# All data transfers issued by SyncE, x and its transpose loaded further ahead, one parameter word for ScalarE, and VectorE's parameter load one step earlier

## Chip, core and metric

The kernel runs on one core of a Trainium2 chip. The time is the device time of one execution in microseconds (us); below it stands as the median of three runs. The profile records one execution of its own.

## What is computed

There are B = 128 items. Each is a matrix x of 128 rows and 512 columns in 32-bit floats, and each goes through four residual stages. The per-item choices are a mask kind (0 to 2), a language (0 to 9), a category (0 to 63) and three scalars zX, zY, zR.

```
h = tanh(x @ W1 + b1); s = h @ v                    # one score for each row
p = softmax(s under the item's mask); x1 = x + (p @ x) / count
a = relu(x1 @ W1[lang] + b1[lang]) @ W2[lang] + b2[lang]
x2 = x1 + layernorm(x1 + a) * gamma[lang] + beta[lang]
x3 = x2 + zX*lap_columns(x2) + zY*lap_rows(x2) + zR*x2*(1 - x2)
out = x3 + x3 @ W[cat] + b[cat]
```

## The kernel before, in words

Every engine runs its own hand-written program of "slots". The loop is unrolled: `run_slots(slot, 0, B + 4)` calls `slot(s)` for s = 0 to 132, and inside one slot an engine works on several items at once, each at another stage (s, s - 1, ... s - 5). The items are sorted by category at the start, so that a category's weights `w3` (1 MB) are loaded only for the first item of a category (`cond=fresh`). Engines wait for each other with semaphores (`wait_ge`), and buffers are rings: three for the transposed x (`xts`), two for x (`xs`), for the category bias (`b3_wide`) and for most others.

**TensorE**, in slot T: the attention projection of item T (`attn_project`, L359), four pieces of the category product of item T - 5 (`category`, L426) with small products between them (L383, L388, L367), the pooling of T - 1 (L395), the transpose of x3 of item T - 4 (`x3_transpose`, L412), the adapter projection of T (L377) and the adapter's second product of T - 1 (`adapter_up`, L404).

**VectorE**, in slot T: `normalize` (L759) of T - 2, mask and row maximum of T, result of T - 5 (L752), `add_b2` (L789) and `add_beta` (L795) of T - 1, the adapter's sum `add_adapted` (L701), the mean (L707), the reaction product (L765), `add_identity` (L727, which TensorE's L388 waits for), columns (L772), epsilon (L744, needs ScalarE's variance L513), `center` (L735), and `add_rows` (L782), which makes x3.

**ScalarE** does tanh (L548), the variance (L513), relu (L529), exponentials (L498), copies, and in the kernel before it also issues three of the transfers: `load_xT` (L564), `load_x` (L578) and `load_b3` (L571). **SyncE** issues the constants (L248 to L253), three row shifts of x2 inside the on-chip memory (`shift_rows`, L276 to L278), the store of the result (L268) and `load_w3` (L262). A transfer waits in the queue of the engine that issues it (q1 is SyncE's, q10 ScalarE's).

SyncE's slot s starts when x2 of item s is there, which VectorE makes in its slot s + 2. SyncE's numbers therefore run two behind those of TensorE.

```
def load_params(eng, what, count, item):
    if item.is_first:
        eng.wait_ge(params_made, 2)
```

ScalarE loads 3 words for each item, VectorE 2, SyncE 4, TensorE twice 1.

Of the kernel before, what the change touches and what calls it, by code (L numbers as in the profile page):

```python
# [12 lines left out]
P = 128  # L13
# [3 lines left out]
FRESH, WSLOT, CAT, ITEM, LANG, KIND, NPARAM = 0, 1, 2, 3, 4, 5, 6  # L17
# [47 lines left out]
def cond_residual_kernel(nc, x, xT, ids, cols, w1a,  # L65
                         w1l, w2l, lrows, gamma, w3, b3, out):
    B, S, D = x.shape
    A = w1a.shape[1] // (D // P)
    K = D // P
# [18 lines left out]
    with ctx:  # L88
# [6 lines left out]
        gamma_wide = sb("gamma_wide", [P, L * D])  # L95
# [34 lines left out]
        xs = sb("xs", [P, 2, D])  # L130
# [115 lines left out]
        def _(sp):  # L246
# [5 lines left out]
            sp.wait_ge(xT_in[0], 16)  # L252
            sp.dma_start(gamma_wide[:, :], gamma.rearrange("l d -> (l d)").partition_broadcast(P)  # L253
                         ).then_inc(gamma_in, 16)

# [24 lines left out]

            words = {}

            def slot(s):
                if s.inside(B):
                    shift_rows(s)
                    words[(s).n] = load_params(sp, FRESH, 4, s)
                if (s - 3).inside(B):
                    store(s - 3, words[(s - 3).n][3])
                if s.inside(B):
                    load_w3(s, words[(s).n][2], words[(s).n][0], words[(s).n][1])  # L290
# [176 lines left out]
        def _(act):  # L467
# [91 lines left out]
            def load_xT(a, item):  # L559
                r = a.ring(3)  # L560
                if a.is_at_least(3):
                    act.wait_ge(xw_mm, a.upto(3))
                    act.wait_ge(attn_mm, a.upto(3))
                act.dma_start(xts[:, r], xT[bass.ds(item, 1)].rearrange("o p (k s) -> p (o k) s", k=K)  # L564
                              ).then_inc(xT_in[r], 16)

            def load_b3(c, cat):
                r = c.ring(2)
                if c.is_at_least(2):
                    act.wait_ge(res_ready, c.upto(2))  # L570
                act.dma_start(b3_wide[:, r], b3[bass.ds(cat, 1)].rearrange("o d -> (o d)").partition_broadcast(P)  # L571
                              ).then_inc(b3_in[r], 16)

            def load_x(d, item):
                r = d.ring(2)
                if d.is_at_least(2):
                    act.wait_ge(pool_mm, d.upto(2))
                act.dma_start(xs[:, r], x[bass.ds(item, 1)].rearrange("o s d -> s (o d)")).then_inc(x_in[r], 16)  # L578

            words = {}  # L580

            def slot(s):
                if s.is_first:
                    words[s.n] = load_params(act, CAT, 3, s)
                    load_xT(s, words[s.n][1])
                if (s + 1).inside(B):
                    words[(s + 1).n] = load_params(act, CAT, 3, s + 1)
                    load_xT(s + 1, words[(s + 1).n][1])
                if s.is_first:
                    load_x(s, words[s.n][1])  # L590
                    for i in range(4, L):
                        move_b2(i)
# [4 lines left out]
                if (s - 1).inside(B) and not (s - 1).is_first:  # L597
                    load_x(s - 1, words[(s - 1).n][1])
                if (s - 2).inside(B):
                    relu(s - 2, words[(s - 2).n][2])  # L600
# [10 lines left out]
                if (s - 4).inside(B):  # L611
                    load_b3(s - 4, words[(s - 4).n][0])
# [7 lines left out]
        def _(dve):  # L620
# [179 lines left out]
            def slot(s):  # L800
# [15 lines left out]
                if (s - 1).inside(B):  # L816
                    add_beta(s - 1, words[(s - 1).n][0])
                    add_adapted(s - 1)
                if (s + 1).inside(B):
                    words[(s + 1).n] = load_params(dve, LANG, 2, s + 1)  # L820
                if (s - 1).inside(B):
                    mean(s - 1)
# [145 lines left out]
```

## Time and profile before

| | us |
|---|---|
| median of 3 runs | 1063.28 (1061.41 to 1067.64) |
| the profiled execution's own time | 1065.58 |
| its span, first to last instruction | 1063.7 |
| TensorE busy (matmul) | 1040.2, 98% |
| VectorE busy | 918.9, 86% |
| ScalarE busy | 480.7, 45% |
| GpSimd busy | 528.2, 50% |

The span is about 2 us shorter than the execution's own time. Busy times leave out waiting and the sequencer's own work (register loads, issuing of transfers). TensorE's granted clock is full in all 40 slices of the page, and the 16 transfer engines moved 253 GB/s in the mean.

### The profile page before, as it was taken

The numbers are of one execution on the slowest core, as the hardware profiler recorded it, in microseconds if no ns is written. First come the engines' busy times: TensorE is split into PE (matmuls) and PEld (weight loads), VectorE is DVE, ScalarE is ACT, GpSimd is POOL, SyncE is SP. The second block draws the span as 40 slices with busy tenths as digits, with TensorE's granted clock in tenths as the row PEclk, the third lists the DMA queues.
The fourth block names the chain that finished last, engine by engine and source line by source line (L and its number), as shares of the span: only waits on it lengthen the run. The fifth ranks groups of instructions, "written<-read, shape, count | busy, mean of one in ns | idle before, by whom it ended". The sixth has DMA issues, their size and how long they took to land.

```text
span 1063.7 us, 22593 instructions
## 1 busy us (share of the span) xinstructions
PE 1040.2 (98%) x4784; PEld 639.1 (60%) x4784; DVE 918.9 (86%) x2216; ACT 480.7 (45%) x1422; POOL 528.2 (50%) x537
## 2 busy tenths in 40 slices
PE   5899999999999999999999999999999999999998
PEld 3566666656665566666665665666666666666663
DVE  5789888988898888988888898889988988988886
ACT  3444444444444444444444454444444444444452
POOL 3345445544544454554454454445454454454454
PEclk9999999999999999999999999999999999999999
DMA  8686898687878978767777778888787888897875
GB/s 332 218 261 212 270 289 258 210 270 231 276 247 263 312 240 264 245 208 240 226 251 223 239 236 254 253 279 279 249 266 254 270 241 275 280 279 235 276 224 176
DMA packets 119109, 268.82 MB, mean 253 GB/s; under 512 B 13010, under 2 KB 13028, under 8 KB 111556
## 3 DMA queue, kind: packets, MB, share of 16 engines
q1 hardware_dynamic: 63428, 166.24, 47.7%
q10 hardware_dynamic: 55552, 101.15, 31.2%
q8 instruction: 47, 0.77, 0.3%
q14 instruction: 82, 0.67, 0.2%
HBM read 243.21 MB, written 33.55 MB: 260 GB/s over the span
## 4 chain that ended last, share of the span: by engine, by line
PE 40%; issue 32%; POOL 21%; DVE 2%; POOLq 0%; ACTq 0%; DVEq 0%; ACT 0%
PE ps_out L426 17%; POOL b_wide L912 8%; POOL rows_near L905 8%; PE bank_hidden L377 5%; PE ps_attn L359 4%; PE ps_adapt L404 4%; PE ps_pool L395 4%; POOL rstd L891 4%; PE ps_x3T L412 2%; POOL neighbours L899 2%; DVE x L759 1%; PE bank_hidden L388 1%; PE bank_scores L367 1%; PE bank_scores L383 1%; DVE x L782 1%
## 5 line engine op out<-in xcount | busy, mean ns | idle before, releaser
L426 PE MATMUL ps_out<-w3s,x3T 128*128 x1016 | 491.7, 593 | 0.8 <-ACT x3T L492 0.8
L899 POOL TENSOR_TENSOR neighbours<-x 128x510 f32<-128x510 f32 x128 | 132.6, 1036 | 191.0 <-DVE x L759 191.0
L426 PEld LDWEIGHTS ps_out<-w3s,x3T 128*128 128x128 f32 x1016 | 164.1, 191 | 101.6 <-issue 101.5
L891 POOL TENSOR_TENSOR rstd<-var_eps,minus_half 128x1 f32<-128x1 f32 x128 | 70.1, 548 | 302.1 <-DVE var_eps L744 302.1
L905 POOL TENSOR_TENSOR rows_near<-rows_near 128x512 f32<-128x512 f32 x128 | 163.2, 1275 | 23.0 <-DMA rows_near<-x 23.0
L359 PEld LDWEIGHTS ps_attn<-xts,w_attn 128*128 128x128 f32 x1024 | 134.3, 191 | 60.8 <-issue 60.8
L912 POOL TENSOR_TENSOR b_wide<-b_wide,x 128x512 f32<-128x512 f32 x128 | 162.9, 1272 | 3.9 <-DMA b_wide<-in_b 3.9
L548 ACT ACTIVATE attn<-ps_attn,vals 128x128 f32<-128x128 f32 x128 | 47.0, 367 | 230.6 <-issue 159.5
L498 ACT ACTIVATE probs<-masked,neg_max 128x128 f32<-128x128 f32 x128 | 51.5, 402 | 216.0 <-DVE neg_max L694 215.9
L377 PE MATMUL bank_hidden<-w_all,xts 128*128 x1024 | 135.4, 275 | 0.1
L359 PE MATMUL ps_attn<-xts,w_attn 128*128 128x128 f32 x1024 | 135.0, 275 | 0.3 <-issue 0.3
L404 PE MATMUL ps_adapt<-w_all,hid 128*128 x256 | 131.2, 594 | 0.5 <-DVE x L759 0.4
L395 PE MATMUL ps_pool<-xs,mixT 128*128 128x512 f32 x256 | 130.7, 592 | 0.0
L377 PEld LDWEIGHTS bank_hidden<-w_all,xts 128*128 128x128 f32 x1024 | 124.5, 192 | 2.0 <-issue 2.0
L412 PEld LDWEIGHTS ps_x3T<-ident,x 128*128 128x128 f32 x512 | 61.3, 141 | 78.3 <-issue 40.5
L701 DVE SCALAR_TENSOR_TENSOR ps_adapt<-ps_adapt,x_b 128x512 f32<-128x512 f32 x128 | 88.9, 694 | 19.6 <-PE ps_adapt L404 18.6
L538 ACT ACTIVATE ps_react<-x,c_t,nzr_t 128x512 f32<-128x512 f32 x128 | 97.8, 764 | 3.8 <-DVE x L782 3.8
L735 DVE SCALAR_TENSOR_TENSOR ps_adapt<-ps_adapt,neg_mean,gamma_wide 128x512 f32<-128x512 f32 x128 | 97.0, 758 | 1.5
L759 DVE SCALAR_TENSOR_TENSOR x<-ps_adapt,rstd,x_beta 128x512 f32<-128x512 f32 x128 | 95.4, 745 | 1.1 <-POOL rstd L891 1.0
L782 DVE SCALAR_TENSOR_TENSOR x<-rows_near,wide_rows,ps_react 128x512 f32<-128x512 f32 x128 | 94.5, 738 | 1.5 <-POOL rows_near L905 1.4
L772 DVE SCALAR_TENSOR_TENSOR ps_react<-neighbours,wide_rows,ps_react 128x512 f32<-128x512 f32 x128 | 95.5, 746 | 0.1
L765 DVE TENSOR_TENSOR ps_react<-ps_react,x 128x512 f32<-128x512 f32 x128 | 88.2, 689 | 0.9 <-ACT ps_react L538 0.9
(111 smaller groups left out, 1306.4 us busy)
## 6 DMA issues: line engine op xcount, KB each, us to landing
w3s<-in_w SPq DMA_DIRECT2D x128, 1024.0 KB
rows_near<-x SPq DMA_DIRECT2D x256, 252.0 KB
xts<-in_xT ACTq DMA_DIRECT2D x128, 256.0 KB, 4.3
xs<-in_x ACTq DMA_DIRECT2D x128, 256.0 KB, 4.5
b_wide<-in_b ACTq DMA_DIRECT2D x128, 256.0 KB, 4.5
out_x<-res SPq DMA_DIRECT2D x128, 256.0 KB, 4.5
w_all<-in_w1l SPq DMA_DIRECT2D x1, 2560.0 KB, 10.4
w_all<-in_w2l SPq DMA_DIRECT2D x1, 2560.0 KB, 16.4
```

Source lines behind the costliest of these rows:

```text
L359: mm = pe.matmul(ps_attn, w1_attn[:, k * A:(k + 1) * A], xts[:, r, k, :], start=(k == 0), stop=(k == K - 1))
L377: mm = pe.matmul(ps_xw, xts[:, s.ring(3), k, :], w1_all[:, bass.ds(lang * (K * A) + k * A, A)], start=(k == 0), stop=(k == K - 1))
L395: pe.matmul(ps_pool[:, :], mixT[:, d.ring(2), :], xs[:, d.ring(2), :], start=True, stop=True).then_inc(pool_mm, 1)
L404: pe.matmul(ps_adapt[:, :], hid[:, g.ring(2), :], w2_all[:, bass.ds(lang * D, D)], start=True, stop=True).then_inc(adapt_mm, 1)
L426: mm = pe.matmul(out_bank(j)[:, :], x3T[:, j.ring(2), k * P:(k + 1) * P], w3s[:, bass.ds(wslot * (K * D) + k * D, D)], start=(k == 0), sto ...
L538: nc.scalar.activation(ps_react[:, :], x2[:, h.ring(2), :], ACT.Identity, bias=c0_t[:, bass.ds(h.n, 1)], scale=nzr_t[:, bass.ds(h.n, 1)]). ...
L759: nc.vector.scalar_tensor_tensor(x2[:, q, :], normed[:, :], rstd[:, q:q + 1], x1_beta[:, q, :], ALU.mult, ALU.add).then_inc(x2_ready, 1)
L782: nc.vector.scalar_tensor_tensor(x3[:, q, :], above[:, q, :], zy_t[:, bass.ds(i.n, 1)], ps_react[:, :], ALU.mult, ALU.add).then_inc(x3_rea ...
L891: nc.gpsimd.tensor_tensor(rstd[:, q:q + 1], var_eps[:, q:q + 1], minus_half[:, :], ALU.pow).then_inc(rstd_ready, 1)
L899: nc.gpsimd.tensor_tensor(neighbours[:, q, 1:D - 1], x2[:, q, 0:D - 2], x2[:, q, 2:D], ALU.add).then_inc(neighbours_ready, 1)
L905: nc.gpsimd.tensor_tensor(above[:, q, :], above[:, q, :], below[:, q, :], ALU.add).then_inc(rows_ready, 1)
L912: nc.gpsimd.tensor_tensor(b3_wide[:, q, :], b3_wide[:, q, :], x3[:, q, :], ALU.add).then_inc(x3_b3_ready, 1)
```

## The change

SyncE now issues every transfer apart from the two constants at the head of ScalarE's program. `load_xT`, `load_b3` and `load_x` move to SyncE with their waits unchanged. SyncE loads its four words six items ahead, the transposed x five of its own slot numbers ahead (three of TensorE's) and x three ahead (one of TensorE's). The `gamma` load (2.5 MB, waits for the first transposed x) comes behind the first six parameter loads, and the transposed x of item 2 and x of item 1 are issued behind `gamma`. ScalarE loads one word (the language) instead of three, two items ahead and behind the variance. VectorE's load of two words moves from behind `add_adapted` to ahead of it.

```diff
@@ SyncE
-            sp.wait_ge(xT_in[0], 16)
-            sp.dma_start(gamma_wide[:, :], gamma.rearrange("l d -> (l d)").partition_broadcast(P)
-                         ).then_inc(gamma_in, 16)
...
+            def load_xT(a, item):
+                r = a.ring(3)
+                if a.is_at_least(3):
+                    sp.wait_ge(xw_mm, a.upto(3))
+                    sp.wait_ge(attn_mm, a.upto(3))
+                sp.dma_start(xts[:, r], xT[bass.ds(item, 1)].rearrange("o p (k s) -> p (o k) s", k=K)
+                              ).then_inc(xT_in[r], 16)
+
+            def load_b3(c, cat):
+                r = c.ring(2)
+                if c.is_at_least(2):
+                    sp.wait_ge(res_ready, c.upto(2))
+                sp.dma_start(b3_wide[:, r], b3[bass.ds(cat, 1)].rearrange("o d -> (o d)").partition_broadcast(P)
+                              ).then_inc(b3_in[r], 16)
+
+            def load_x(d, item):
+                r = d.ring(2)
+                if d.is_at_least(2):
+                    sp.wait_ge(pool_mm, d.upto(2))
+                sp.dma_start(xs[:, r], x[bass.ds(item, 1)].rearrange("o s d -> s (o d)")).then_inc(x_in[r], 16)
+
             words = {}
+            for i in range(6):
+                words[i] = load_params(sp, FRESH, 4, Step(i))
+                if i < 2:
+                    load_xT(Step(i), words[i][3])
+                if i == 0:
+                    load_x(Step(i), words[i][3])
+            sp.wait_ge(xT_in[0], 16)
+            sp.dma_start(gamma_wide[:, :], gamma.rearrange("l d -> (l d)").partition_broadcast(P)
+                         ).then_inc(gamma_in, 16)
+
+            load_xT(Step(2), words[2][3])
+            load_x(Step(1), words[1][3])
+            load_xT(Step(3), words[3][3])
+            load_x(Step(2), words[2][3])
+            load_xT(Step(4), words[4][3])
 
             def slot(s):
                 if s.inside(B):
                     shift_rows(s)
-                    words[(s).n] = load_params(sp, FRESH, 4, s)
+                if (s + 5).inside(B):
+                    load_xT(s + 5, words[(s + 5).n][3])
+                if (s + 3).inside(B):
+                    load_x(s + 3, words[(s + 3).n][3])
+                if (s - 1).inside(B):
+                    load_b3(s - 1, words[(s - 1).n][2])
                 if (s - 3).inside(B):
                     store(s - 3, words[(s - 3).n][3])
+                if (s + 6).inside(B):
+                    words[(s + 6).n] = load_params(sp, FRESH, 4, s + 6)
                 if s.inside(B):
                     load_w3(s, words[(s).n][2], words[(s).n][0], words[(s).n][1])
@@ ScalarE (its own load_xT, load_b3, load_x are removed)
             def slot(s):
                 if s.is_first:
-                    words[s.n] = load_params(act, CAT, 3, s)
-                    load_xT(s, words[s.n][1])
-                if (s + 1).inside(B):
-                    words[(s + 1).n] = load_params(act, CAT, 3, s + 1)
-                    load_xT(s + 1, words[(s + 1).n][1])
-                if s.is_first:
-                    load_x(s, words[s.n][1])
+                    words[s.n] = load_params(act, LANG, 1, s)
+                    words[(s + 1).n] = load_params(act, LANG, 1, s + 1)
                     for i in range(4, L):
                         move_b2(i)
                 if (s - 1).inside(B):
                     attn_tanh(s - 1)
                 if (s - 3).inside(B):
                     variance(s - 3)
-                if (s - 1).inside(B) and not (s - 1).is_first:
-                    load_x(s - 1, words[(s - 1).n][1])
+                if (s + 2).inside(B):
+                    words[(s + 2).n] = load_params(act, LANG, 1, s + 2)
                 if (s - 2).inside(B):
-                    relu(s - 2, words[(s - 2).n][2])
+                    relu(s - 2, words[(s - 2).n][0])
...
-                if (s - 4).inside(B):
-                    load_b3(s - 4, words[(s - 4).n][0])
@@ VectorE
                     add_beta(s - 1, words[(s - 1).n][0])
-                    add_adapted(s - 1)
                 if (s + 1).inside(B):
                     words[(s + 1).n] = load_params(dve, LANG, 2, s + 1)
+                if (s - 1).inside(B):
+                    add_adapted(s - 1)
                 if (s - 1).inside(B):
                     mean(s - 1)
```

## Rows read from the trace of the kernel before

**Rows 1.** The page: busy us of each engine (share) and instructions

```profile
PE 1040.2 (98%) x4784; PEld 639.1 (60%) x4784; DVE 918.9 (86%) x2216; ACT 480.7 (45%) x1422; POOL 528.2 (50%) x537
```

**Rows 2.** Timeline (start, us, engine, line): four starts of TensorE's slots

```profile
50.04 1.05 PE L359 MATMUL ps_attn<-xts,w_attn 128*128 128x128 f32 x8
...
501.23 1.05 PE L359 MATMUL ps_attn<-xts,w_attn 128*128 128x128 f32 x8
...
509.17 1.05 PE L359 MATMUL ps_attn<-xts,w_attn 128*128 128x128 f32 x8
...
1028.43 1.05 PE L359 MATMUL ps_attn<-xts,w_attn 128*128 128x128 f32 x8
```

**Rows 3.** Waits of the whole span: us in total, times, longest us

```profile
ACT attn L548 <- issue: 159.5, 77, 3.1
...
DVE neg_mean L707 <- issue: 33.9, 28, 1.5
...
DVE var_eps L744 <- ACT square_junk L513: 26.2, 57, 1.2
...
SPq L262 <- PE ps_out L426: 292.3, 126, 3.4
```

**Rows 4.** All parameter loads (L238): ns min/median/max, first and last start

```profile
L238 PEldq TENSOR_LOAD <-all_params x256: 293/298/493, 20.9 to 1054.7; - x128
L238 ACTq TENSOR_LOAD <-all_params x128: 698/1374/2881, 14.6 to 1012.5; - x128
L238 DVEq TENSOR_LOAD <-all_params x128: 522/1080/2589, 21.3 to 1028.6; - x128
L238 SPq TENSOR_LOAD <-all_params x128: 816/1531/2757, 36.9 to 1049.6; - x128
```

**Rows 5.** Timeline of an ordinary slot

```profile
508.34 0.67 DVE L795 TENSOR_TENSOR x_beta<-ps_pool,beta_wide 128x512 f32<-128x512 f32 x1
...
509.37 0.70 DVE L701 SCALAR_TENSOR_TENSOR ps_adapt<-ps_adapt,x_b 128x512 f32<-128x512 f32 x1 [0.35 <-PE ps_adapt L404]
...
510.51 0.15 DVE L707 TENSOR_SCALAR neg_mean<-y_sum 128x1 f32<-128x1 f32 x1 [0.39 <-DVE ps_adapt L701]
...
513.02 0.74 DVE L782 SCALAR_TENSOR_TENSOR x<-rows_near,wide_rows,ps_react 128x512 f32<-128x512 f32 x1
...
514.48 0.14 PEld L412 LDWEIGHTS ps_x3T<-ident,x 128*128 128x128 f32 x1 [0.24 <-issue]
```

**Rows 6.** Timeline of a long slot

```profile
73.99 0.67 DVE L795 TENSOR_TENSOR x_beta<-ps_pool,beta_wide 128x512 f32<-128x512 f32 x1
...
74.58 0.69 DVE L701 SCALAR_TENSOR_TENSOR ps_adapt<-ps_adapt,x_b 128x512 f32<-128x512 f32 x1
...
76.70 0.15 DVE L707 TENSOR_SCALAR neg_mean<-y_sum 128x1 f32<-128x1 f32 x1 [1.37 <-issue]
```

**Rows 7.** The long slot's VectorE parameter load

```profile
L238 DVEq TENSOR_LOAD <-all_params x1: 2471/2471/2471, 74.2 to 74.2; - x1
```

**Rows 8.** Stretches: us, busy per engine (PE, PEld, DVE, ACT, POOL), clock, DMA share, GB/s

```profile
507.00:508.00 1.00, 1.00 (x11) 1.00 (x10) 1.00 (x3) 0.98 (x3) 1.00 (x2) 1.00 0.00 0
508.00:509.00 1.00, 1.00 (x7) 0.69 (x6) 1.00 (x3) 0.86 (x3) 1.00 (x2) 1.00 0.56 184
```

**Rows 9.** Timeline of the start

```profile
19.09 0.33 SPq L253 DMA_DIRECT2D gamma_wide<-in_gamma  x1
...
21.82 0.34 ACTq L564 DMA_DIRECT2D xts<-in_xT  x1
...
30.38 1.05 PE L359 MATMUL ps_attn<-xts,w_attn 128*128 128x128 f32 x8
...
32.75 0.76 DVE L735 SCALAR_TENSOR_TENSOR ps_adapt<-ps_adapt,neg_mean,gamma_wide 128x512 f32<-128x512 f32 x1
```

**Rows 10.** Transfers of 14 to 30 and 20 to 24 us: KB, us to landing

```profile
gamma_wide<-in_gamma SPq DMA_DIRECT2D x1, 2560.0 KB, 9.9
...
xts<-in_xT ACTq DMA_DIRECT2D x1, 256.0 KB, 7.5
```

More of the change, by code:

```diff
@@ L557, in column_ends @@
                                      ).then_inc(edges_ready, 1)
[L559 to L578, printed above, removed]
             words = {}
```

## The prediction

> **What bounds the kernel now.** I read the page first. TensorE's matmuls are busy for 98% of the span, VectorE for 86% and ScalarE for 45% [rows 1]. That says that TensorE is close to the bound, not how close. So the second view is the timeline at the starts of TensorE's slots. An ordinary slot is 509.17 - 501.23 = 7.94 us, and in it the matmuls follow each other without a gap. From the start of slot 5 (50.04) to that of slot 127 (1028.43) there are 122 slots in 978.4 us. At 7.935 each they would take 968.1 [rows 2]. The excess is 10.3 us, and that is all that any change to waits can win in the steady state. What lies before 50.04 and behind 1028.43 is the ramp and the tail.
>
> The third view is the waits. TensorE's gaps come from VectorE's results (mixT for L388, x3 for L412). What holds VectorE is not an engine: 28 times the mean (L707) waited with the cause "issue", 33.9 us in all, up to 1.5, and ScalarE's tanh did so 77 times, 159.5 us [rows 3]. The fourth view says what the sequencers did then. A parameter load takes VectorE 0.52 us at best, 1.08 in the median and 2.59 at worst, ScalarE's three words 0.70, 1.37 and 2.88, while TensorE's single word takes 0.30 nearly always [rows 4]. The last view is an ordinary slot beside a long one. In the ordinary one the sum (L701) starts at 509.37, when TensorE has delivered, and the mean at 510.51 [rows 5]. In the long one the sum starts at 74.58, but the mean only at 76.70, after a load of 2.47 us [rows 6, 7]. The long slots follow the long loads, and those fall where the transfer engines are full. So the kernel is bound by TensorE plus 10.3 us in which a register load holds VectorE, or ScalarE, too long.
>
> **ScalarE's part.** It loses three transfers for each item and two of three words, and its load moves behind the variance, where the next instruction (relu) waits for TensorE anyway. Tanh and variance then start when their data are there. This ends most of the wait of epsilon for the variance, 26.2 us in 57 waits [rows 3]. No row shows one word on ScalarE. Its bounds are TensorE's 0.30 from below and three words' 1.37 from above; I take 0.5, since TensorE's row has the same count. The cover is over 1 us in an ordinary slot, so it costs nothing. At 1.37 or more, without that cover, relu would be up to 0.4 late, and its reader (`adapter_up`) comes 2 us later still.
>
> **VectorE's part.** The load before stood behind the sum and ran beside it. Two cases have to be told apart.
>
> Case one, VectorE waits for TensorE (ordinary slot). Before, the load started with the sum at 509.37, so the mean came at 509.45 + d for a load of length d, and at 510.16 without a stall (a sum and its accumulator read, 0.79). Now the load starts with L795 at 508.34, and everything up to the wait is cover.
>
> Case two, VectorE is behind (long slot). The sum followed L795 by 0.59, the load began at 74.2 and the mean stood idle for 1.37 us after a load of 2.47 [rows 6, 7], that is d - 1.1. Now the sum itself stands behind the load and begins at about d + 0.1 instead of 0.59 after L795. The stall is d - 0.5, so it is 0.6 us worse than before.
>
> The cover now: VectorE's busy time for each item is 918.9 / 128 = 7.18 us, of which a little belongs to the set-up; with 7.1 a slot of 7.94 leaves 0.8 for a stall, so loads up to 0.8 + 0.5 = 1.3 us cost nothing. Lateness is carried on: a slot starts late by what the last left over, plus d, minus 1.3, never under zero. TensorE notices when the lateness passes some limit. In the ordinary slot x3 is finished at 513.02 + 0.74 = 513.76 and its reader loads weights at 514.48 [rows 5], with a mean that was 0.35 late already, so the limit is 0.72 + 0.35, about 1.05 us.
>
> What d will be is the open number. It starts up to 1 us earlier than now. At 507 to 508 the transfer engines are idle, and at 508 to 509 they are at 0.56 [rows 8], so the load mostly runs before the row shifts and `w3` fill them. With a quiet engine 0.52 is shown, so ordinary loads should be some 0.7. Where a new category's weights follow at once on those of the last, the engines are full throughout, and nothing shortens it: up to 2.59. I take 1.5 for those with `w3` in flight. Then one such load is 0.2 late, a following ordinary one makes up 0.6, and only runs of several reach the limit. Remaining excess: at best 0; with today's lengths kept (ordinary loads 1.08 recover 0.2, long ones of 1.8 to 2.5 lose 0.5 to 1.2) about what it was, 8 to 10. I take 3, nearer to the lower end as the load leaves the full stretch. Gain 10.3 - 3 = 7.3 us, bounds 10.3 and 0.
>
> **SyncE in the steady state.** It gains three issues, each 0.34 us plus 0.1 for addresses and waits: 1.4 us a slot, and its load of up to 2.76 [rows 4] stays. It waits for the category product before issuing `w3` for 292.3 us in 126 slots, 2.3 each [rows 3]. The 1.4 us fit, so `w3` and the shifts behind it are issued when they were. Passed are: shifts first, then transposed x, x, bias, store, parameters, `w3`. The transposed x is needed two TensorE slots after its issue (about 15 us), x and bias over 6; even the one caught beside `gamma` took 7.5 [rows 10]. Cost zero, with that cover; without it each late microsecond would be TensorE's.
>
> **The start.** Here the change costs. Before, `gamma` was issued at 19.09, transposed x of item 2 at 21.82 in the other queue [rows 9]; they landed at 19.09 + 9.9 = 29.0 and 21.82 + 7.5 = 29.3 [rows 10]. TensorE took the latter at 30.38 and VectorE gamma at 32.75 [rows 9]. Now SyncE runs six loads of four words first. From 14.6, when ScalarE's first load starts [rows 4]: 6 x 0.9 (0.82 is SyncE's minimum; the queue is nearly idle) and three issues of 0.4 give 14.6 + 5.4 + 1.2 = 21.2, with one or two loads slowed by traffic 22. `gamma` lands at 22 + 9.4 = 31.4 (half a microsecond shorter, as nothing shares with it), before 32.75. The transposed x of item 2 stands in the same queue behind it, 0.7 us more: about 32.1, 1.7 later than 30.38. Everything behind is a chain (tanh of item 2 stands ahead of item 0's variance on ScalarE), so I carry 1.7 in full. Below: loads at the minimum and half of it made up in the ramp, 0.5. Above: loads at the median 1.53 give `gamma` 4 us later, so 5. In the ramp VectorE is behind and its load costs 0.3 more a slot, ScalarE's shorter load gives as much back: zero.
>
> From the Trainium skill, "DMA: Bandwidth & Descriptors", section "Queues, rings and completion order": each transfer engine takes a queue's descriptors in order and alternates between queues packet by packet. By alternation the small transfer of item 2 should have passed `gamma` by far, and here it landed 0.3 behind it; by the first half of the rule it now stands wholly behind `gamma`, as I have it. The sum would be 1.7 us smaller if the queue did not keep order.
>
> **The tail.** The same semaphores order the last shifts, biases and stores, and the last product is TensorE's. Zero, bounds -0.8 (no bias load beside the last shift) and +0.5.
>
> **Sum.** -7.3 + 1.7 = -5.6 us. The profiled execution's own time is 1065.58, its span 1063.7; the median of the runs is 1063.28, within 2.3 of the first. The excess does not depend on that difference, so 1063.3 - 5.6 = 1057.7, say 1058.
>
> **Rivals.** *The load is no shorter (A).* It starts later again whenever VectorE is late, and then meets the full engines as now. Excess left 8, start +1.7: 1063.3 - 2.3 + 1.7 = 1062.7. For it: 1.08 in the median with engines at 0.56 share. Against: 0.52 is shown where they are quiet.
>
> *Slower: the sum behind the load makes VectorE the bound (B).* A slot of VectorE alone is 7.1 + d - 0.5. It passes 7.94 at a mean d of 1.34, and each 0.1 above costs 122 x 0.1 = 12 us. At a mean of 1.4 it is 7 us over the floor, plus 5 for the unevenness, with the start 1063.3 - 10.3 + 12 + 1.7 = 1066.7; at 1.45, 1073. For it: loads of 2.5 us exist, and nothing covers them now. Against: the median is 1.08, and each late start only reaches today's phase.
>
> *A heavy start (C).* SyncE's loads take 1.5 us: 1063.3 - 7.3 + 5 = 1061.
>
> *All gaps close (D).* 1063.3 - 10.3 + 0.5 = 1053.5.
>
> *It does nothing (E).* The Trainium skill, same page, section "Issuing engines are not separate DMA queues", says that issuing from several engines saves only the sequencer's time to issue, mostly small. By that ScalarE's three issues were never in the way. As a mechanism here: 3 x 0.34 us on an engine that is busy 45%, all hidden, and the start alone counts: 1063.3 + 1.7 = 1065.
>
> **Numbers.** Forecast 0.42, A 0.2, B 0.12, C 0.08, D 0.13, E 0.05. The range 1053 to 1067 takes in the forecast's own bounds (1054 to 1061), A, C, D, E and half of B. A measurement of this kernel tells some 0.5% (5.3 us) from nothing, so faster is under 1058.0: all of D, most of half the forecast, some of C and A's luck, 0.42 x 0.65 + 0.13 + 0.04 = 0.44; slower is over 1068.6: part of B, 0.1; the rest, 0.46.
>
> **What the profile will show.** Right: slot starts of TensorE at 7.94 with few over 8.2; "issue" gone from tanh; the mean no longer waiting for issue, the sum doing so at times instead; VectorE's median load well under 1.08; epsilon's wait for the variance gone; `gamma` issued near 22, attention of item 2 near 32. Wrong if VectorE's loads stay at 1.1 or more with the sum idle behind them in most slots, if L426 waits for `w3`, or if slot 5 starts later than 52.

## The result, and the profile after

The changed kernel took 1053.32 us in the median of 7 runs (1052.18 to 1058.22). The kernel before took 1067.39 (1061.41 to 1068.84, 7 runs) beside it. The ratio is 0.9889, with a 95% interval from 0.9862 to 0.9916: the change makes the kernel 1.1% faster. (The ratio is estimated from all the runs; the two medians alone give 0.9868, inside the interval.) The profiled execution has a span of 1051.6 us, 12.1 less than before.

The page's busy line hardly moves against [rows 1]. TensorE's 1031.5 is 8.7 lower, and its share of the span is 98% as before:

```profile
PE 1031.5 (98%) x4784; PEld 641.8 (61%) x4784; DVE 913.4 (87%) x2216; ACT 487.7 (46%) x1422; POOL 531.0 (50%) x537
```

TensorE's slot starts in the timeline (start, us, engine, line), the answer to [rows 2]:

```profile
48.61 1.05 PE L398 MATMUL ps_attn<-xts,w_attn 128*128 128x128 f32 x8
...
500.86 1.05 PE L398 MATMUL ps_attn<-xts,w_attn 128*128 128x128 f32 x8
...
1017.20 1.05 PE L398 MATMUL ps_attn<-xts,w_attn 128*128 128x128 f32 x8
```

From slot 5 to slot 127 it is 1017.20 - 48.61 = 968.6 us. At 7.935 a slot, 122 slots take 968.1, so the excess is 0.5 us, where it was 10.3. The difference of the spans comes apart in three: -9.8 us in the steady state, -1.4 before slot 5 (50.04 to 48.61), -0.9 behind the start of slot 127 (35.3 to 34.4).

The waits of the whole span (us, times, longest), the answer to [rows 3]:

```profile
ACT attn L587 <- PE ps_attn L398: 142.7, 123, 1.2
...
DVE ps_adapt L712 <- PE ps_adapt L443: 62.5, 118, 0.5
...
DVE var_eps L755 <- ACT square_junk L552: 1.3, 2, 0.7
...
SPq L258 <- PE ps_out L465: 167.2, 120, 3.1
```

Tanh waits for TensorE now, in 123 slots, and never for issue. The mean's wait for issue is gone from the view, and so is all but 1.3 us of epsilon's wait for ScalarE. SyncE still waits 1.4 us a slot for the category product (before 2.3).

The parameter loads, the answer to [rows 4]:

```profile
L238 PEldq TENSOR_LOAD <-all_params x256: 294/299/535, 20.3 to 1042.8; - x128
L238 SPq TENSOR_LOAD <-all_params x128: 295/878/1919, 14.4 to 996.9; - x128
L238 ACTq TENSOR_LOAD <-all_params x128: 276/285/1998, 14.4 to 994.6; - x128
L238 DVEq TENSOR_LOAD <-all_params x128: 522/532/1597, 20.7 to 1015.8; - x128
```

VectorE's median fell from 1.08 to 0.53, ScalarE's from 1.37 to 0.28. An ordinary slot in the timeline, the answer to [rows 5], now with ScalarE's rows, for they turn out to be what counts:

```profile
500.86 1.05 PE L398 MATMUL ps_attn<-xts,w_attn 128*128 128x128 f32 x8
...
501.95 0.37 ACT L587 ACTIVATE attn<-ps_attn,vals 128x128 f32<-128x128 f32 x1 [1.19 <-PE ps_attn L398]
502.21 0.68 ACT L552 ACTIVATE square_junk<-ps_adapt,neg_mean 128x512 f32<-128x512 f32 x1
...
503.78 0.15 DVE L755 TENSOR_SCALAR var_eps<-var_sum 128x1 f32<-128x1 f32 x1
...
504.50 0.74 DVE L793 SCALAR_TENSOR_TENSOR x<-rows_near,wide_rows,ps_react 128x512 f32<-128x512 f32 x1
...
506.17 0.14 PEld L451 LDWEIGHTS ps_x3T<-ident,x 128*128 128x128 f32 x1 [0.24 <-issue]
```

Reckon from the slot's start, 500.86. Tanh runs at 1.09, at once when attention is done. The square follows, epsilon runs at 2.92, x3 is finished at 505.24, and TensorE reads it at 5.31, so 0.93 us lie between. (The fillers of the next section measure a margin of 1.1.)

Now the long slot of the kernel before again [rows 6], with ScalarE's rows, which the prediction had not looked at, first its register load and then the timeline:

```profile
L238 ACTq TENSOR_LOAD <-all_params x1: 2757/2757/2757, 74.1 to 74.1; - x1
```

```profile
74.40 0.39 ACT L522 ACTIVATE mix<-probs,scale 128x128 f32<-128x128 f32 x1
...
77.09 0.34 ACTq L564 DMA_DIRECT2D xts<-in_xT  x1
...
77.54 0.37 ACT L548 ACTIVATE attn<-ps_attn,vals 128x128 f32<-128x128 f32 x1 [2.74 <-issue]
...
77.81 0.68 ACT L513 ACTIVATE square_junk<-ps_adapt,neg_mean 128x512 f32<-128x512 f32 x1
...
78.61 0.15 DVE L744 TENSOR_SCALAR var_eps<-var_sum 128x1 f32<-128x1 f32 x1 [0.30 <-ACT square_junk L513]
...
80.23 0.42 PEld L412 LDWEIGHTS ps_x3T<-ident,x 128*128 128x128 f32 x4 [0.87 <-DVE x L782]
```

ScalarE's load began at 74.1 and took 2.76 us. Then came the issue of the transposed x, and only then, 3.70 behind the slot's start (73.84), tanh. Epsilon started at 4.77, held by the square and not by the late mean of [rows 6]. TensorE stood idle for x3, and the slot took 8.64 us.

Epsilon's start behind TensorE's slot start, slot by slot for slots 5 to 125, can be set against what the slot's length is over 7.935, the excess. Worked out from the traces of five kernels, three of them of the next section, that gives one table (us):

| epsilon starts at | before | VectorE's load alone | ScalarE's load alone | transfers alone | changed |
|---|---|---|---|---|---|
| under 4.0: slots, excess in all | 92, -0.1 | 83, -0.1 | 116, 0.0 | 113, 0.0 | 121, 0.5 |
| 4.0 to 4.2: slots, mean excess | 10, 0.07 | 12, 0.07 | 5, 0.12 | 7, 0.11 | none |
| 4.2 to 4.4 | 6, 0.24 | 8, 0.24 | none | 1, 0.28 | none |
| over 4.4 | 13, 0.63 | 18, 0.62 | none | none | none |

Up to 4.0 us nothing happens; beyond, the slot gets longer by about what epsilon starts later than that. In the kernel before the 29 late slots make up the whole excess: 0.7 + 1.4 + 8.3 = 10.4 us. The 0.5 us that the changed kernel keeps have another chain. They lie in slots 110 and 111, where GpSimd, which makes `rstd` from epsilon, had waited 3.12 us for a row shift to land and 1.74 us for the bias, so that VectorE waited for it:

```profile
887.92 0.75 DVE L770 SCALAR_TENSOR_TENSOR x<-ps_adapt,rstd,x_beta 128x512 f32<-128x512 f32 x1 [1.84 <-POOL rstd L903]
```

### The profile page after: what moved, and what is told of

Its sections match the earlier page's. It is cut to its first block and busy times, and to the rows that moved or that the text cites. A ratio compares the mean times of both kernels' runs of the same rounds, so it can differ in the third digit from the quotient of the medians.

```text
span 1051.6 us, 22463 instructions
## 1 busy us (share of the span) xinstructions
PE 1031.5 (98%) x4784; PEld 641.8 (61%) x4784; DVE 913.4 (87%) x2216; ACT 487.7 (46%) x1422; POOL 531.0 (50%) x537
## 5 line engine op out<-in xcount | busy, mean ns | idle before, releaser
L924 POOL TENSOR_TENSOR b_wide<-b_wide,x 128x512 f32<-128x512 f32 x128 | 162.7, 1271 | 44.3 <-DMA b_wide<-in_b 44.1
L917 POOL TENSOR_TENSOR rows_near<-rows_near 128x512 f32<-128x512 f32 x128 | 163.2, 1275 | 38.7 <-DMA rows_near<-x 38.3
L568 ACT ACTIVATE hid<-bank_hidden,vals 128x128 f32<-128x128 f32 x128 | 47.0, 368 | 245.3 <-PE bank_hidden L427 245.2
L537 ACT ACTIVATE probs<-masked,neg_max 128x128 f32<-128x128 f32 x128 | 51.6, 403 | 139.6 <-DVE neg_max L705 139.6
L451 PEld LDWEIGHTS ps_x3T<-ident,x 128*128 128x128 f32 x512 | 63.7, 141 | 69.2 <-issue 65.1
```

What stands on the lines that cost most here:

```text
L917: nc.gpsimd.tensor_tensor(above[:, q, :], above[:, q, :], below[:, q, :], ALU.add).then_inc(rows_ready, 1)
L924: nc.gpsimd.tensor_tensor(b3_wide[:, q, :], b3_wide[:, q, :], x3[:, q, :], ALU.add).then_inc(x3_b3_ready, 1)
```

## The experiments

All ratios are to the kernel before, run on the same chip in the same session, so the medians of different sessions are not to be compared. The kernel before had a median of 1067.39 us beside the first run of the changed kernel, 1069.46 beside the two kernels with one load moved, the one with both and the one with all but VectorE's load, 1069.30 beside the second run of the changed kernel, the transfers alone, the one word and gamma last, and 1065.22 beside the fillers and the transposed x behind the square. "Excess" is TensorE's time from slot 5 to slot 127, less 968.1, in the profiled execution.

| kernel | median us | ratio (95%) | excess | start of slot 5 | slot 127 to end |
|---|---|---|---|---|---|
| before, as in the profile of rows 2 | 1063.28 | 1 | 10.3 | 50.0 | 35.3 |
| changed, first | 1053.32 | 0.9889 (0.9862 to 0.9916) | 0.5 | 48.6 | 34.4 |
| changed, again | 1055.43 | 0.9875 (0.9847 to 0.9902) | -0.1 | 52.4 | 34.4 |
| VectorE's load alone | 1070.09 | 1.000 (0.998 to 1.002) | 13.9 | 53.6 | 35.2 |
| ScalarE's load alone | 1056.81 | 0.9869 (0.9841 to 0.9897) | 0.5 | 51.8 | 35.0 |
| both loads, not the transfers | 1056.36 | 0.9873 (0.9847 to 0.9899) | 0.2 | 51.0 | 35.2 |
| transfers alone | 1056.20 | 0.9885 (0.9857 to 0.9912) | 1.0 | 49.9 | 34.4 |
| all but VectorE's load | 1057.35 | 0.9879 (0.9851 to 0.9906) | 1.8 | 51.3 | 34.4 |
| one word in front of tanh | 1054.98 | 0.9873 (0.9845 to 0.9900) | 1.3 | 49.5 | 34.4 |
| gamma last | 1054.88, one run | - | -0.1 | 50.7 | 34.4 |
| filler in front | 1079.83 | 1.0128 (1.0100 to 1.0156) | 22.5 | 51.9 | 36.2 |
| longer filler in front | 1240.80 | 1.1647 (1.1615 to 1.1678) | 175.0 | 54.5 | 40.5 |
| filler behind tanh | 1097.87 | 1.0313 (1.0283 to 1.0344) | 40.7 | 49.7 | 36.3 |
| transposed x behind the square | 1062.17 | 0.9971 (0.9954 to 0.9988) | 3.9 | 56.1 | 35.1 |

**VectorE's load alone** (kernel before, one move):

```diff
                     add_beta(s - 1, words[(s - 1).n][0])
-                    add_adapted(s - 1)
                 if (s + 1).inside(B):
                     words[(s + 1).n] = load_params(dve, LANG, 2, s + 1)
+                if (s - 1).inside(B):
+                    add_adapted(s - 1)
```

> The kernel before with one edit: VectorE's parameter load stands ahead of the adapter's sum; ScalarE keeps its three words and its transfers. Theory P (place): a load is slow where it meets the row shifts and the category weights, which start to move some 1.3 us after their issue, so the early load is short, 0.53 us in the median as in the changed kernel, the mean no longer waits, and 6 to 8 of the 10.3 us of excess between slot 5 and slot 127 go; ratio 0.992 to 0.994. Theory O (overlap): the loads of ScalarE, VectorE and SyncE hinder each other, as they start within half a microsecond. VectorE's then comes first and is short too: the same here. Rival of my prediction (the sum stands behind a long load): median 1.1 or more, excess 8 or more, ratio 1.0 or above. In all three ScalarE's three words stay at 1.37 and epsilon still waits for the variance in some slots.

It gives nothing. The waits of this kernel show why:

```profile
ACT attn L548 <- issue: 162.4, 77, 3.5
...
DVE var_eps L744 <- ACT square_junk L513: 54.1, 55, 1.9
```

The mean's wait for issue is gone, and epsilon waits for ScalarE instead, 54.1 us where it was 26.2. VectorE comes to epsilon earlier (3.02 us behind the slot's start in the median, before 3.14; 3.25 at the 90th percentile, before 3.93), and epsilon starts hardly earlier in the median and later at the 90th percentile (3.21 and 4.63; before 3.26 and 4.44). The load's length changed as well: in the 43 slots in which it ran beside ScalarE's alone its median was 0.88 us, in the 61 in which nothing ran beside it 0.54. Theories P and O both had 6 to 8 us of excess going with this move; none went, and both fall here as accounts of the loss.

**ScalarE's load alone.** In the kernel before, its load of three words moves behind the variance (an item further ahead); nothing else.

```diff
                 if s.is_first:
                     words[s.n] = load_params(act, CAT, 3, s)
                     load_xT(s, words[s.n][1])
-                if (s + 1).inside(B):
                     words[(s + 1).n] = load_params(act, CAT, 3, s + 1)
+                if (s + 1).inside(B):
                     load_xT(s + 1, words[(s + 1).n][1])
...
                     variance(s - 3)
+                if (s + 2).inside(B):
+                    words[(s + 2).n] = load_params(act, CAT, 3, s + 2)
```

> The kernel before with one edit: ScalarE's load of three words goes behind the variance and one item further ahead; its transfers and VectorE's load stay. Theory P: VectorE's load stays at 1.08 in the median with a maximum over 2.3, and of the 10.3 us of excess some 3 go (tanh and variance on time). Theory O: VectorE's load loses its neighbour of 0.27 us ahead and falls to 0.6 to 0.8 in the median, and 7 or more of the excess go.

This one edit gives the whole gain. Tanh starts at 1.09 in the median (before 2.19), and epsilon's wait is down to 1.3 us in 2 times. The next row is as bad as ever and costs nothing:

```profile
DVE neg_mean L709 <- issue: 42.7, 34, 1.6
```

Neither theory had this. P had only 3 us going, and O had them go because VectorE's load would get shorter; its median was 1.20 us, longer than before.

**Both loads, without the transfers**, and **all but VectorE's load** (the changed kernel with that load behind the sum again, the first diff turned round):

> The kernel before with both loads moved (ScalarE's three words behind the variance, VectorE's ahead of the sum), and every transfer left where it was. If the loads alone hold VectorE and TensorE back, as both theories P and O say, the excess falls under 1.5 us and the ratio is 0.989 to 0.991, within the interval of the changed kernel. If moving the transfers to SyncE has a share of its own in the steady state (theory T), 2 us or more of excess stay. The start (slot 5 at 50.0) and the tail (35.3) should stay as before, as their gain of 1.4 and 0.9 us is put down to the transfers.

> The changed kernel with VectorE's load put back behind the adapter's sum; one word on ScalarE, all transfers on SyncE. Here ScalarE's load starts 1 us behind VectorE's and SyncE's 2.5 us behind, so nothing overlaps it. Theory P: its place meets shifts and weights as before, median 1.0 to 1.1, up to 2.5, the mean waits for issue in some 20 to 30 slots, 4 to 7 us of excess come back; ratio to the kernel before 0.993 to 0.996. Theory O: the load stays at 0.53, excess under 1.5 and ratio 0.988 to 0.990, as for the changed kernel.

The first has 0.2 us of excess, so theory T, which kept 2 us or more for the transfers, falls. The second has 1.8: VectorE's load is at 0.88 us again and the mean waits 44.8 us for issue in 34 waits, much as P said, but the 4 to 7 us that P had coming back do not come. The medians of these two and of ScalarE's load alone lie within 1.0 us, so VectorE's load is worth less than what these runs tell apart. Nor do the transfers have to move.

**The changed kernel again, and the transfers alone.** For the second, ScalarE's load of three words stands ahead of tanh again and VectorE's behind the sum; SyncE issues the transfers.

```diff
+                if (s + 2).inside(B):
+                    words[(s + 2).n] = load_params(act, CAT, 3, s + 2)
                 if (s - 1).inside(B):
                     attn_tanh(s - 1)
...
-                if (s + 2).inside(B):
-                    words[(s + 2).n] = load_params(act, LANG, 1, s + 2)
```

> The changed kernel itself once more, beside the next three, so that its ratio to the kernel before is known with one chip's runs: 0.988 to 0.990 is expected by all theories, some 10 to 12.5 us below the kernel before. In the profile the steady state from slot 5 to slot 127 should be within 1 us of 122 x 7.935 = 968.1 again. Open is how far the start to slot 5 (48.6 there, 50.0 to 53.6 in five other profiles) repeats: theory C (chance) says that it comes out anywhere from 48.5 to 51.5, theory S (the earlier issue of gamma and of the transposed x) that it stays under 49.

> All transfers issued by SyncE as in the change, but ScalarE's load of three words ahead of tanh and VectorE's load behind the sum, as before: the transfers' part of the change alone. Theory L (the gain is the removal of ScalarE's register load from in front of tanh and variance): the excess over 7.935 us a slot comes back to 8 to 14 us, and only the shorter tail (-0.8) and perhaps a shorter start are left: ratio 0.997 to 1.001. Theory T (the transfers on one queue, six slots of words ahead, do part of it, because ScalarE then has three issues less in the way): half of the 10 us of excess goes, ratio about 0.994.

The first repeats the gain (0.9875, excess -0.1). Its slot 5 starts at 52.4, so theory S falls, and the spread by chance is wider than C had it.

The second result overthrew my theory L, and T had half of it only. The transfers alone give all of the gain too, with ScalarE's load just as long as before and VectorE's at 0.88 in the median (before 1.08):

```profile
L238 ACTq TENSOR_LOAD <-all_params x128: 702/1350/3529, 14.5 to 995.5; - x128
L238 DVEq TENSOR_LOAD <-all_params x128: 524/878/2429, 21.5 to 1019.2; - x128
```

The waits of this kernel:

```profile
DVE neg_mean L718 <- issue: 36.1, 28, 1.7
...
DVE var_eps L755 <- ACT square_junk L552: 4.2, 11, 0.8
```

So the load as such is no fault. The same slot 8 in this kernel's timeline starts at 73.71, with a load of 2.66 us on ScalarE from 73.7 and one of 2.20 on VectorE:

```profile
76.49 0.37 ACT L587 ACTIVATE attn<-ps_attn,vals 128x128 f32<-128x128 f32 x1 [2.07 <-issue]
76.75 0.68 ACT L552 ACTIVATE square_junk<-ps_adapt,neg_mean 128x512 f32<-128x512 f32 x1
...
77.70 0.15 DVE L755 TENSOR_SCALAR var_eps<-var_sum 128x1 f32<-128x1 f32 x1
```

Tanh comes at 2.78 instead of 3.70 and epsilon at 3.99 instead of 4.77, just on the limit, and the slot takes 7.99 us. The 0.92 us that tanh gained are 0.57 because no transfer is issued between the load's end and tanh (0.67 us before, 0.10 now), 0.25 because the load starts earlier (over all slots half a microsecond: at -0.55 from the slot's start in the median, before -0.04; the issues of x and of the bias, which stood ahead of it in ScalarE's program, are gone), and 0.1 because it is shorter. That suggested a margin rather than a culprit (theory M): anything that takes some 0.8 us away ahead of the square should do.

**One word in front of tanh.** The changed kernel, with ScalarE's `load_params` of one word moved ahead of `attn_tanh`.

> The changed kernel, but ScalarE's load of one word stands at the head of its slot ahead of tanh, where the three words stood before. Theory N (the length counts: three words of 1.4 us in the median, up to 2.9, are too long there, one word is not): the one word takes 0.3 to 1.1 us, tanh starts that much later, the slack of a slot takes it, excess 0 to 2 us, ratio 0.988 to 0.991. Theory P (the place counts: what stands ahead of tanh meets the traffic of w3 and holds the chain from tanh over variance to x3 whatever it loads): loads of over 1.5 us in slots with fresh w3, excess over 4 us, ratio 0.992 or more.

N is right: loads of 0.49 in the median and 1.39 at most, started at -0.56, delay tanh hardly ever (1.09 in the median and at the 90th percentile), and no time is lost.

**Fillers.** One more ScalarE copy in each slot puts a number on the margin.

```diff
+                if (s - 4).inside(B):
+                    act.wait_ge(w1_in, 16)
+                    nc.scalar.activation(idle_junk[:, :], w1_all[:, 0:2560], ACT.Copy)
                 if (s - 1).inside(B):
                     attn_tanh(s - 1)
```

> The changed kernel with one more ScalarE instruction in each slot from the fourth: a copy of 2560 columns that nobody reads, ahead of tanh. Its price is estimated from the rows of 512 columns (575 ns) and 128 (276 ns): 2.2 us. Theory M (margin: a slot gets longer only by what epsilon starts later than 4.0 us behind the slot's start): ScalarE is free at -0.1, so tanh starts at 2.1 instead of 1.09, the square ends at 3.1 instead of 2.1, epsilon starts near 3.2: below the limit, so the excess from slot 5 to 127 stays under 2 us and the time within 2 us of the changed kernel's (ratio 0.986 to 0.991). Theory E (each microsecond ahead of tanh lengthens the chain from attention to x3): 122 slots by up to 1.0 us, over 20 us more, ratio over 1.005.

> The same with 4096 columns, estimated at 3.4 us. Theory M: tanh starts at 3.3, the square ends at 4.35, epsilon starts near 4.4, which is 0.35 to 0.4 past the limit in every slot: 122 times that is 43 to 49 us, ratio 1.025 to 1.04. Theory R (it is the register loads that hurt, by holding a sequencer while transfers are in flight, not ScalarE being late): ScalarE is busy 45% and takes 3.4 us more without loss, ratio under 0.995.

> The copy of 2560 columns between tanh and the square instead of ahead of tanh. Theory V (it is the square, and through it epsilon, that comes late): tanh starts at 1.09 as in the changed kernel, the square ends at about 1.4 + 2.2 + 0.9 = 4.45, epsilon starts near 4.5, 0.4 to 0.5 past the limit in every slot: 50 to 60 us more, ratio 1.035 to 1.05. Theory H (it is tanh, for which TensorE's attention scores wait): nothing changes against the changed kernel, ratio under 0.995.

The copies took 2.33 and 3.61 us. The last of the three in the timeline, one slot and the start of the next:

```profile
504.51 1.05 PE L399 MATMUL ps_attn<-xts,w_attn 128*128 128x128 f32 x8
505.60 0.37 ACT L588 ACTIVATE attn<-ps_attn,vals 128x128 f32<-128x128 f32 x1
...
505.87 2.33 ACT L611 ACTIVATE idle_junk<-w_all 128x2560 bf16<-128x2560 f32 x1
...
508.09 0.68 ACT L553 ACTIVATE square_junk<-ps_adapt,neg_mean 128x512 f32<-128x512 f32 x1
...
508.89 0.15 DVE L759 TENSOR_SCALAR var_eps<-var_sum 128x1 f32<-128x1 f32 x1 [1.17 <-ACT square_junk L553]
...
510.52 0.42 PEld L452 LDWEIGHTS ps_x3T<-ident,x 128*128 128x128 f32 x4 [0.93 <-DVE x L797]
...
512.77 1.05 PE L399 MATMUL ps_attn<-xts,w_attn 128*128 128x128 f32 x8
```

Tanh is on time at 1.09, the square is late, epsilon starts at 4.38, and the slot takes 8.26 us, 0.33 over. Theory V stands and H falls: it is the square and not tanh. V's figure of 50 to 60 us more was too high, as epsilon came at 4.38 and not at 4.5; it was some 40. R, by which ScalarE would take the longer filler without loss, falls with a ratio of 1.165. The three fillers measure the limit, if a slot gets longer by just what epsilon is past it. With epsilon at 4.23, 4.38 and 5.51 in the median the mean slot was 0.18, 0.33 and 1.43 us over, so the limit is 4.05, 4.05 and 4.08.

What failed was my estimate of where the filler in front would start. I had ScalarE free at -0.1. In fact tanh started at 3.17 and 4.45, so both fillers began at 0.94. A late epsilon makes VectorE's row maximum late (6.69 us behind the slot's start in the median, changed kernel 5.28), ScalarE's exponentials wait for that (305 us in all, changed kernel 139.6), and the delay comes round to the next slot's head. So the first filler, which M had below the limit, came past it, and the total agrees with theory E's figure of over 20 us. What speaks against E are the kernel with one word in front and the transfers alone, where up to a microsecond and more ahead of tanh costs next to nothing. With the longer filler TensorE also waited for tanh itself (attention scores, 108.8 us in 124 times), so the 4.08 of that kernel is no clean reading of the limit; the other two have 1.1 us of this wait at most.

**The transposed x behind the square** (kernel before, one move):

```diff
                 if (s + 1).inside(B):
                     words[(s + 1).n] = load_params(act, CAT, 3, s + 1)
-                    load_xT(s + 1, words[(s + 1).n][1])
...
                     variance(s - 3)
+                if (s + 1).inside(B):
+                    load_xT(s + 1, words[(s + 1).n][1])
```

> The kernel before with one edit: ScalarE issues the transposed x behind the variance instead of between its load of three words and tanh; everything else, VectorE's load too, stays. In the kernel before tanh starts 0.85 us after the end of the load, in the one with the transfers alone moved 0.3 after it. Theory M: tanh and the square come 0.5 us earlier; of the 30 slots of the kernel before in which epsilon started after 4.0 (mean 0.35 past it, up to 1.0) most fall under the limit, and the excess falls from 10 to 14 us to 2 to 4: ratio 0.990 to 0.993. Theory Q (the loads' lengths and the queue decide, not half a microsecond of issuing): ratio 0.998 to 1.002.

The excess is 3.9, inside M's range: tanh's median is 1.49 (before 2.19), and only 2 slots have epsilon after 4.0, where it was 29. They give 0.5 us of the excess; the other 3.3 lie in slots with epsilon in time. In the longest of these, 0.99 over at 733.3, GpSimd had waited 4.5 us for a row shift and VectorE 1.0 for GpSimd's `rstd`, as in the changed kernel's slots 110 and 111; for the others the cause stays open. The ratio of 0.9971 is neither M's (0.990 to 0.993) nor Q's (0.998 to 1.002). The edit has a price at the start, which I had overlooked: slot 5 starts at 56.1, 6.1 later than before and outside the 48.6 to 53.6 of the ten profiles above the fillers in the table. The transposed x of item 1 is issued later, beside gamma, and TensorE waits for it:

```profile
20.46 0.34 ACTq L564 DMA_DIRECT2D xts<-in_xT  x1
...
28.60 1.65 PE L359 MATMUL ps_attn<-xts,w_attn 128*128 128x128 f32 x6 [4.68 <-DMA xts<-in_xT]
```

**Gamma last.** The changed kernel with the transposed x of item 2 and x of item 1 issued ahead of gamma.

```diff
+            load_xT(Step(2), words[2][3])
+            load_x(Step(1), words[1][3])
             sp.dma_start(gamma_wide[:, :], gamma.rearrange("l d -> (l d)").partition_broadcast(P)
                          ).then_inc(gamma_in, 16)
-            load_xT(Step(2), words[2][3])
-            load_x(Step(1), words[1][3])
```

> The changed kernel with the transposed x of item 2 and x of item 1 issued ahead of gamma at the start. If one queue's transfers are served in the order of issue, the transposed x of item 2 lands about 4 to 5 us earlier than its 29.30 and gamma some 0.6 to 1 us later than 28.62; if they share the engines packet by packet, hardly anything moves. For the time both say nothing measurable: in the profile of the changed kernel TensorE took that item at 29.34, right behind its own work, so that nothing waited, and VectorE takes gamma only after 31: within 1 us of the changed kernel in the start to slot 5, apart from chance.

Two stretches of its transfers (KB, us to landing):

```profile
xts<-in_xT SPq DMA_DIRECT2D x1, 256.0 KB, 2.6
...
gamma_wide<-in_gamma SPq DMA_DIRECT2D x1, 2560.0 KB, 11.0
```

Ahead of gamma the small transfer, issued at 20.30, lands at 22.95, 6.35 us earlier than behind it (29.30). So the queue does work in order of issue, in this one run. Gamma, issued at 21.16 and so 1.4 later, lands at 32.2, 3.6 later than in the changed kernel, which is more than I had expected. The start to slot 5 (50.7) is in the middle of the others.

## Why the prediction came out as it did

The time lay in the range given, and 1.1% is on the "faster" side. But the likeliest forecast, -5.6 us, was half of the -12.1 between the profiles. The steady state went by rival D, to which I had given 0.13. The measured 1053.32 is 0.3 us above the lower end of the range, and the sum behind the forecast came true in neither term. The -7.3 us were the worth of VectorE's shorter load, and that move alone is worth nothing (ratio 1.000, 0.998 to 1.002). The +1.7 us of the start came out as -1.4. That the time still fell in the range, on the right side, was luck as far as this mechanism goes: the change also had the move that counts, and I had named it without a price. Point by point:

**The view of what bounds the kernel.** The 10.3 us of excess as the most that waits can give was right: 9.8 came back, and 10.4 in a second profile of the changed kernel. Wrong was the step from the third and fourth view, "in which a register load holds VectorE, or ScalarE, too long", for I then priced VectorE's half only. The load on VectorE held the mean 33.9 us in 28 waits, and that is unpaid: with 36.1 and 42.7 us of the same wait the excess is 1.0 and 0.5. The row that named the cause was in [rows 3] too, epsilon waiting for the square, 26.2 us in 57 times. I mentioned it as a by-product of "ScalarE's part" and gave it no term.

**Case two and the cover.** "Lateness is carried on", with its 3 us of remaining excess, was mis-sized; 0.5 and -0.1 were measured. The limit I had derived for it, 1.05 us over the ordinary slot, was good: epsilon ordinarily starts at 2.92 to 2.93 and the fillers put the limit at 4.05 to 4.08, 1.1 later. It applies to epsilon, whoever makes it late.

**The lengths of the loads.** VectorE's I put at 0.7 in ordinary slots and 1.5 with `w3` in flight. It was 0.53 in nearly all. "The engines are full throughout, and nothing shortens it" fails: at 1.06 us behind the issue of `w3` the transfer engines were 0.7 busy in the median and the load was at its minimum. ScalarE's one word took 0.28 in the median, under my lower bound of 0.30, and 2.0 at most, over my upper one of 1.37. It did cost nothing, as said, even in front of tanh.

**SyncE in the steady state.** Right: zero. Its wait for the category product shrank by 1.0 us a slot, of the 1.4 that I had charged, and some of the rest went into shorter loads (0.88 in the median, before 1.53). Not foreseen: GpSimd waits 44.1 us for the bias, 53 times (before 3.9, once), and 38.3 for the shifted rows (before 23.0). In the profile of the changed kernel this costs only the 0.5 us of slots 110 and 111.

**The start.** Wrong in size and sign. Gamma was issued at 19.78 and not near 22; rows of the changed kernel's timeline:

```profile
19.78 0.34 SPq L306 DMA_DIRECT2D gamma_wide<-in_gamma  x1
20.32 0.33 SPq L282 DMA_DIRECT2D xts<-in_xT  x1
...
29.35 1.16 PE L398 MATMUL ps_attn<-xts,w_attn 128*128 128x128 f32 x8
...
31.83 0.76 DVE L746 SCALAR_TENSOR_TENSOR ps_adapt<-ps_adapt,neg_mean,gamma_wide 128x512 f32<-128x512 f32 x1
```

The six loads took 0.49, 0.89, 0.31, 0.87, 0.29 and 0.87 us, 3.7 together, where I had taken 0.9 each from SyncE's minimum in [rows 4]. From there the reckoning held: gamma took 8.8 us to land (9.4 forecast), the transposed x landed at 29.30, 0.7 behind it as said, and TensorE's matmul took it at 29.35 with no gap behind the one before; only its weight load had waited, 0.85 us. How much of the -1.4 belongs to the change can't be told. In the ten profiles above the fillers in the table slot 5 starts at 48.6 to 53.6, and the changed kernel itself did so at 48.6 and 52.4. In the second of these TensorE's granted clock was 0.50 (1.2 GHz) from 23.0 to 27.7, in the kernel with gamma last 1.00 (2.4 GHz) from 22 to 30. So "slot 5 later than 52" was no sign of this change: the changed kernel has it both ways.

The order of the queue was as I had used it, and the kernel with gamma last shows it (the small transfer lands 6.35 us earlier when issued ahead of gamma): this agrees with the first half of the rule cited from the Trainium skill, "DMA: Bandwidth & Descriptors", section "Queues, rings and completion order".

**The tail.** I had zero with -0.8 as the bound. It is 0.6 to 0.9 shorter in all six kernels in which SyncE issues the transfers and no filler runs (34.4, against 35.0 to 35.3 in the five others). The cause wasn't looked for.

**The rivals.** A falls with VectorE's load at 0.53. B, VectorE as the bound, needed a mean load of 1.34 us, which never came. C, a heavy start, falls with 3.7 us for SyncE's six loads. E had looked at ScalarE's issues. The Trainium skill, same page, section "Issuing engines are not separate DMA queues", says that issuing from several engines saves only the sequencer's time, which is usually small beside the transfer. These runs agree: with the transfers left on ScalarE the gain is the same, and an issue takes 0.34 us where a transfer takes 4.5. What E made of it fails. I had priced 3 x 0.34 us on an engine that is busy 45% as hidden; taking them away alone gives 1.15% (0.9885, 0.9857 to 0.9912), because they stood ahead of the square, whose margin was used up. Small beside the transfer isn't small beside a margin.

In sum, what the runs show: in 29 of the 121 slots of the kernel before, ScalarE's queue of load, issue, tanh and square ended too late for epsilon, and those slots were 0.36 us too long in the mean. Moving the load takes 1.4 us out of that queue in the median, moving the transfers 0.9 in slot 8, and either is enough alone. They don't add up, because beyond the limit there is nothing left to win. No version tried is faster than the changed kernel by more than these runs can tell: the ratios of the changed kernel and five others lie between 0.9869 and 0.9889, with intervals that overlap, and the smallest edit among them is the move of ScalarE's load.

## What to carry to other kernels

Price a wait by the chain that ends in the bounding engine, and not by its own length: set the start of each link against the bounding engine's slot start, for all slots, and look for the point from which the slot gets longer. Here 34 us of idle VectorE cost nothing, and the whole loss of 10 us stood behind another wait of 26 us. Where several edits take time out of one queue, the first may bring all of the gain, as here.

## What the runs showed of the hardware

The length of a register load depends on more than its words. Four words took SyncE 0.82 at least in the kernel before and 0.29 to 0.89 at the start of the changed one. ScalarE's three words, at the same place, took 2.31 us in the median of the 53 slots in which fresh `w3` was on its way and 1.31 in the 69 others; one word went from 0.28 to 2.00. TensorE's stayed at 0.30 in nearly every case. VectorE's two words took 0.53 when they ran alone early in the slot and 0.88 beside ScalarE's. What sets these lengths was not settled: the runs show only that here they don't decide the time.
